# First attention of a two-layer block: both visible triangles of the 128-token window share 128 columns in the softmax

## The reference, cut to what matters

```python
q = jnp.einsum('btd,ndh->btnh', x, q_kernel)          # N = 16 heads of H = 128
kv = jnp.einsum('bsd,ckdh->cbskh', x, kv_kernel)      # K = 8 groups
k, v = (kv[0], kv[1])
q = apply_rope(rms_norm(q, q_norm_scale), positions)
k = apply_rope(rms_norm(k, k_norm_scale), positions)
mask = (j <= i) & (i - j < 128)                       # WINDOW = 128
logits = jnp.einsum('btkgh,bskh->bkgts', qg * ATTN_SCALE, k)
probs = jax.nn.softmax(jnp.where(mask, logits, finfo.min), axis=-1)
enc = jnp.einsum('bkgts,bskh->btkgh', probs, v)
return jnp.einsum('btnh,nhd->btd', enc, out_kernel)
```

## Time and profile before

| | us |
|---|---|
| three runs | 1667.22, 1682.62, 1681.39 |
| median | 1681.39 |
| span of the profiled execution (first to last instruction) | 1677.7 |
| TensorE (PE) busy | 1563.1 (93%) |
| VectorE (DVE) busy | 1115.7 (67%) |
| ScalarE (ACT) busy | 863.7 (51%) |
| GpSimd (POOL) busy | 402.9 (24%) |
| mean granted TensorE clock | 0.945 of full |

### The profile page before, as it was taken

One profiled execution on the slowest core, in us unless ns is written; L12 is line 12 of the kernel. 1 busy time (PEld: TensorE's weight loads), 2 busy tenths in 40 slices (PEclk: granted clock), 3 DMA queues, 4 the chain that ended last, 5 costly groups with the idle time before them and its releaser, 6 DMA issues.

```text
span 1677.7 us, 24009 instructions
## 1 busy us (share of the span) xinstructions
PE 1563.1 (93%) x7538; PEld 1139.9 (68%) x7582; DVE 1115.7 (67%) x2452; ACT 863.7 (51%) x2004; POOL 402.9 (24%) x473
## 2 busy tenths in 40 slices
PE   4999999899999998999999999996999999999898
PEld 3888788778878886677777777774544445444366
DVE  7997798589858983775555555544664756647554
ACT  4777677667766774443323223222443544435466
POOL 4665666466646652000000000000000000000000
PEclk9999999999999998999999999997877989869899
DMA  6000000000000002320000000003000000000001
GB/s 223 2 1 1 1 2 1 3 1 1 1 3 1 2 1 51 96 85 19 1 1 0 0 0 0 0 0 116 1 1 1 1 0 0 0 0 0 0 14 38
DMA packets 15769, 28.04 MB, mean 17 GB/s; under 512 B 2000, under 2 KB 10064, under 8 KB 15152
## 3 DMA queue, kind: packets, MB, share of 16 engines
q1 hardware_dynamic: 15264, 25.98, 4.6%
q0 software_dynamic: 400, 0.78, 0.2%
HBM read 25.44 MB, written 2.10 MB: 16 GB/s over the span
## 4 chain that ended last, share of the span: by engine, by line
PE 74%; DVE 10%; issue 6%; POOL 5%; ACT 4%; DMA 1%; DVEq 0%; ACTq 0%; SPq 0%; POOLq 0%
PE ps L1121 13%; PE ps L1123 13%; PE ps L1122 12%; PE ps L1379 5%; PE ps L1451 4%; PE ps L1174 4%; PE ps L1220 4%; PE ps L1439 4%; PE ps L1426 2%; PE ps L1235 2%; POOL rope L385 2%; PE ps L1512 2%; PE ps L1201 1%; DVE ssum L525 1%; PE ps L1276 1%
## 5 line engine op out<-in xcount | busy, mean ns | idle before, releaser
L1043 ACT ACTIVATE pT<-ps 128x512 f32<-128x512 f32 x256 | 146.1, 597 | 213.9 <-PE ps L1439 212.8
L357 POOL TENSOR_TENSOR ln_rs<-ln_ve,minus_half 128x4 f32<-128x4 f32 x16 | 17.4, 1085 | 978.4 <-DVE ln_ve L421 978.4
L715 DVE TENSOR_REDUCE nm<-ps 128x1 f32<-128x512 f32 x256 | 168.7, 685 | 59.0 <-PE ps L1379 57.5
L1121 PE MATMUL ps<-xnT_lo,w1moe_hi 128*128 128x512 f32 x400 | 178.1, 445 | 2.0 <-DVE w2moe_lo L662 1.8
L974 ACT ACTIVATE moe_act_hi<-sg 128x512 fp32r<-128x512 f32 x100 | 63.3, 633 | 190.5 <-DVE sg L639 190.5
L1122 PE MATMUL ps<-xnT_hi,w1moe_lo 128*128 128x512 f32 x400 | 161.1, 403 | 0.0
L1123 PE MATMUL ps<-xnT_hi,w1moe_hi 128*128 128x512 f32 x400 | 160.0, 400 | 0.0
L385 POOL TENSOR_TENSOR rope<-rope 128x384 f32<-128x384 f32 x128 | 144.3, 1127 | 0.0
L1379 PE MATMUL ps<-kst,qst 64*128 64x512 f32 x256 | 130.1, 526 | 13.3 <-DVE nm L715 7.2
L629 DVE TENSOR_TENSOR sg<-ps,sg 128x512 f32<-128x512 f32 x100 | 69.0, 690 | 97.2 <-ACT sg L994 97.1
L1121 PE MATMUL ps<-wqkv_lo,xnT_hi 128*128 128x512 f32 x256 | 122.1, 477 | 8.6 <-issue 5.6
(11 more groups left out here) (204 smaller groups left out, 3800.1 us busy)
## 6 DMA issues: line engine op xcount, KB each, us to landing
yT<-in_w1moe SPq DMA_DIRECT2D x25, 256.0 KB, 2.6
encT<-in_wqkv SPq DMA_DIRECT2D x8, 512.0 KB, 9.0
w_in<-in_w2moe SPq DMA_DIRECT2D x25, 128.0 KB, 2.7
wo<-in_wo SPq DMA_DIRECT2D x1, 2048.0 KB, 19.5
wm<-in_wm SPq DMA_DIRECT2D x2, 1024.0 KB, 10.8
out_x<-x_res SPq DMA_DIRECT2D x4, 512.0 KB, 2.9
x_res<-in_x SPq DMA_DIRECT2D x1, 1536.0 KB, 15.1
pT<-in_c_pick SPq DMA_DIRECT2D x1, 1024.0 KB, 5.8
```

Source lines behind the costliest of these rows:

```text
L715: V.tensor_reduce(nm1[:, m % 2, t, col:col + 1], ps[:, 2 + i % 2, :], AX.X, ALU.max, negate=True).then_inc(s1_max, 1)
L1043: A(pT1[:, u % 2, 2 * (m % 2) + h, c, :], ps[:, 4 + i % 2, :], ACT.Exp, scale=SCALE1).then_inc(p1_ready, 1)
L1121: MM(out, left[0], right[1], start=first, stop=False)
```

## The change

The two triangles are disjoint, so both fit into 128 columns for the softmax. Scores of a tile with an older triangle: no `window` matmul; the older and the causal products go to two halves of the bank, and VectorE overwrites the causal half where key > query with the older half (`copy_predicated` with the integer mask `older`). Maximum, exponential, normalisation and turning then work on 128 columns a head, always. After turning and copying, GpSimd parts the result again into two zero-filled matrices (`probT_parts`) by two `affine_select` instructions of 128 x 256, and TensorE multiplies each with the values of its tile. A first tile has only the causal triangle, keeps its mask matmul, and needs no parting. VectorE's wait for the scores moves ahead of the reciprocal, and the normalisation becomes one `tensor_tensor`. SP loads one more constant (`older`, 128 KB), and the DMA of `window` becomes that of `causal`.

```diff
@@ gpsimd, attention_step
+                m = n - 7
+                older_too = new and 0 <= m < STEPS and m % TT > 0
+                if older_too:
+                    pool.wait_ge(probT_ready, b * STEPS + m + 1)
+                    if m >= 2:
+                        pool.wait_ge(attended, b * STEPS + m - 1)
                 for h in heads[0:1]:
                     split_weights(h)
+                if older_too and n >= STEPS and not heads:
+                    nc.gpsimd.tensor_tensor(idle[:], minus_half[:, 0:1], minus_half[:, 0:1], ALU.add)
...
                     nc.gpsimd.tensor_tensor(msq[:, s, :], ssum[:, s, :], eps_sum[:], ALU.add).then_inc(meaned, 1)
+                if older_too:
+                    q = m % 2
+                    nc.gpsimd.affine_select(probT_parts[:, q, 0], probT[:, q], [[0, 2], [-1, P]], ALU.is_gt, 0.0,
+                                            base=0, channel_multiplier=1)
+                    nc.gpsimd.affine_select(probT_parts[:, q, 1], probT[:, q], [[0, 2], [1, P]], ALU.is_ge, 0.0,
+                                            base=0, channel_multiplier=-1).then_inc(probT_split, 1)
@@ vector, attention_step
-                    for h in range(2):
-                        ins = V.tensor_scalar(prob[:, m % PROB_RING, h, 0:w], prob[:, m % PROB_RING, h, 0:w], rsums[:, s, h:h + 1],
-                                              None, ALU.mult)
+                    if m % TT:
+                        V.copy_predicated(bank[:, :, 1, :], older[:], bank[:, :, 0, :]).then_inc(merged, 1)
...
+                    V.tensor_tensor(prob[:, m % PROB_RING], prob[:, m % PROB_RING],
+                                    rsums[:, s, :].unsqueeze(2).to_broadcast((P, 2, P)), ALU.mult).then_inc(probn_ready, 1)
...
-                    V.tensor_reduce(nmax[:, s, :], ps[:, 3 + s, :].rearrange("p (h f) -> p h f", h=2)[:, :, 0:w],
-                                    AX.X, ALU.max, negate=True).then_inc(max_ready, 1)
+                    V.tensor_reduce(nmax[:, s, :], bank[:, :, 1, :], AX.X, ALU.max, negate=True).then_inc(max_ready, 1)
@@ scalar, attention_step
-                    kt = slice(1, 4, 2) if m % TT == 0 else slice(0, 4)
-                    A(probT[:, s, kt, :], ps[:, 5, :].rearrange("p (a f) -> p a f", a=4)[:, kt, :], ACT.Copy
+                    A(probT[:, s], ps[:, 5, 0:2 * P].rearrange("p (h f) -> p h f", h=2), ACT.Copy
...
-                        ins = A(prob[:, m % PROB_RING, h, 0:w], ps[:, 3 + s, h * 2 * P:h * 2 * P + w], ACT.Exp,
+                        ins = A(prob[:, m % PROB_RING, h, :], ps[:, 3 + s, (2 * h + 1) * P:(2 * h + 2) * P], ACT.Exp,
@@ tensor, attention_step
-                    pe.wait_ge(probT_ready, k + 1)
+                    if t == 0:
+                        pe.wait_ge(probT_ready, k + 1)
+                    else:
+                        pe.wait_ge(probT_split, b * OLDER_STEPS + with_older(m))
...
-                    else:
-                        MM(ps[:, 3 + s, :], ident_b[:], window[:].rearrange("p h a f -> p (h a f)"),
-                           start=True, stop=False, skip_group_check=True)
...
-                        for part in ((1,) if t == 0 else (0, 1)):
-                            at = 0 if t == 0 else part * P
-                            ins = T(ps[:, 5, (2 * h + part) * P:(2 * h + part + 1) * P],
-                                    prob[:, m % PROB_RING, h, at:at + P], ident[:])
+                        ins = T(ps[:, 5, h * P:(h + 1) * P], prob[:, m % PROB_RING, h, :], ident[:])
```

More of the change, by code:

```diff
@@ L19 @@
 AX = mybir.AxisListType
+I32 = mybir.dt.int32
 P = 128
@@ L97, in build @@
         ident_b = sb("ident_b", [P, P], BF16, part_a)
-        window = sb("window", [P, 2, 2, P], BF16, part_a)
+        idle = sb("idle", [P, 1], where=part_a)
+        causal = sb("causal", [P, 2, P], BF16, part_a)
+        older = sb("older", [P, 2, P], I32, part_a)
         qks = sb("qks", [P, 3, P], where=part_a)
@@ L109, in build @@
         rsums = sb("rsums", [P, 2, 2], where=part_a)
-        prob = sb("prob", [P, PROB_RING, 2, 2 * P], where=part_a)
-        probT = sb("probT", [P, 2, 4, P], where=part_a)
+        prob = sb("prob", [P, PROB_RING, 2, P], where=part_a)
+        probT = sb("probT", [P, 2, 2, P], where=part_a)
+        probT_parts = sb("probT_parts", [P, 2, 2, 2, P], where=part_a)
         encT = sb("encT", [P, HEADS0, SEQ], where=part_a)
@@ L211, in build @@
         wd_loaded = sem("wd_loaded")
-        masks_loaded = sem("masks_loaded")
+        masks_loaded, older_loaded = sem("masks_loaded"), sem("older_loaded")
         out_stored = sem("out_stored")
@@ L280, in heads_next @@
             return (OLD_HEADS_AT.get(n + 1, ()), -1) if old else ((), 0)
+        with_older = lambda m: 3 * (m // TT) + m % TT
+        OLDER_STEPS = GROUPS * (TT - 1)
         weighted_tile = lambda j: -1 if j == 0 else j - 2 if j >= 2 else None
@@ L314, in _ @@
                     sp.dma_start(sin_in, dram["c_sin"]).then_inc(tables_loaded, 16)
+                    sp.dma_start(older[:], dram["c_older"]).then_inc(older_loaded, 16)
             sp.dma_start(x_res[:, TT:NTILES, :], dram["x"][1:BATCHES].rearrange("b (t p) d -> p (b t) d", p=P)
@@ L380, in attention_step @@
                     nc.gpsimd.tensor_tensor(msq[:, s, :], ssum[:, s, :], eps_sum[:], ALU.add).then_inc(meaned, 1)
+                if older_too:
[4 more added lines that the diff above has]
+                                            base=0, channel_multiplier=-1).then_inc(probT_split, 1)
+                if new and n < STEPS:
+                    k, s = b * STEPS + n, n % 2
                     pool.wait_ge(meaned, k + 1)
@@ L918, in attention_step @@
                     m = n - 4
-                    k, s, w = k0 + m, m % 2, (P if m % TT == 0 else 2 * P)
+                    k, s = k0 + m, m % 2
                     act.wait_ge(max_ready, k + 1)
@@ L1173, in attention_step @@
                     for part in parts:
+                        weights = probT[:, s] if t == 0 else probT_parts[:, s, part]
                         ins = MM(ps[:, 6, 0:2 * P], raw[:, (m - 1 + part) % RAW_RING, 3 * P:4 * P],
-                                 probT[:, s, part::2, :], start=part == parts[0], stop=part == 1)
+                                 weights.rearrange("p h f -> p (h f)"), start=part == parts[0], stop=part == 1)
                     ins.then_inc(attended, 1)
@@ L1209, in attention_step @@
                         pe.wait_ge(prob_ready, k - 1)
-                    bank = ps[:, 3 + s, :].rearrange("p (h f) -> p h f", h=2)
+                    bank = ps[:, 3 + s, :].rearrange("p (h a f) -> p h a f", h=2, a=2)
                     if t == 0:
-                        MM(bank[:, :, 0:P], ident_b[:], window[:, :, 1, :], start=True, stop=False,
-                           skip_group_check=True)
-                    else:
-                        MM(ps[:, 3 + s, :], ident_b[:], window[:].rearrange("p h a f -> p (h a f)"),
-                           start=True, stop=False, skip_group_check=True)
+                        MM(bank[:, :, 1, :], ident_b[:], causal[:], start=True, stop=False, skip_group_check=True)
                     for h in range(2):
                         for part in ((1,) if t == 0 else (0, 1)):
-                            at = 0 if t == 0 else part * P
-                            ins = MM(bank[:, h, at:at + P], qkT[:, m % QK_RING, h, :],
-                                     qkT[:, (m - 1 + part) % QK_RING, 2, :], start=False,
+                            ins = MM(bank[:, h, part, :], qkT[:, m % QK_RING, h, :],
+                                     qkT[:, (m - 1 + part) % QK_RING, 2, :], start=t > 0 and h == 0 and part == 0,
                                      stop=h == 1 and part == 1, skip_group_check=True)
@@ L1619 @@
     qi, kj = np.arange(P)[:, None], np.arange(P)[None, :]
-    masks = np.where(np.stack([kj > qi, kj <= qi], 1), np.float32(0), np.float32(-1e30))
-    arrays["c_window"] = np.ascontiguousarray(np.broadcast_to(masks[:, None], (P, 2, 2, P)))
+    masks = np.where(kj <= qi, np.float32(0), np.float32(-1e30))
+    arrays["c_causal"] = np.ascontiguousarray(np.broadcast_to(masks[:, None], (P, 2, P)))
+    arrays["c_older"] = np.ascontiguousarray(np.broadcast_to((kj > qi).astype(np.int32)[:, None], (P, 2, P)))
     feat = np.arange(FT * P)
```

30 lines of the change are left out of this document (21 added, 9 removed).

## The result

The changed kernel takes 1849.54 us (median of 4 runs, 1841.18 to 1860.08) against 1677.43 (1667.22 to 1682.62) for the kernel before, by runs of both on the same chip: ratio 1.1044, 95% interval 1.0973 to 1.1115. The forecast was 1933 in a range of 1835 to 2035. The profiled execution took 1852.63 us with a span of 1850.9, which is 173.2 above the span of before.

What follows compares the result with a forecast made beforehand. TensorE was taken to bound the first attention, until selections close a longer loop through four engines. 1681.4 + 215 for the loop - 10 outside its stretches + 47 for the clock = 1933 us, range 1835 to 2035.

Steps and rivals of the forecast that it cites:

- the loop: First attention: projection, copy, square, sum, msq, two selections, product, next projection; 4.91 + 2S us an interval against today's 4.13.
- the stretches: First attention, steps 8 to 31 of each batch: groups of four tiles take 24.27 instead of 15.31 us, +215 us.
- rival 1: First attention: selections cheap and clock holds; 1833 us with S = 0.57, 1855 with S = 0.725; chance 0.22.
- the clock: TensorE's granted clock falls after pauses in half of the 72 long intervals: +47 us, bounds nothing to +150.
- S: Time of one GpSimd selection, two per tile with an older triangle: taken as 0.94 us.
- the short interval: Fourth interval of a group, with a first tile's product and no selections to wait for: 3.9 us.
- Outside the stretches: Steps 0 to 7 and 32 to 39: 24 tiles save 0.43 us each, -10 us; +10 if cover is gone.
- What the change removes: TensorE, 96 tiles with an older triangle: mask and two turns, 0.43 us a tile, 41 us if TensorE stayed the bound.
- VectorE at nothing: VectorE's edits, with copy_predicated taken as 0.42 us, sum to -0.2 us, at worst +0.2; costed at nothing.
- faster: First attention: selections are hidden and TensorE keeps its pace less 0.43 us a tile, 1640 us; chance 0.02.
- the clock falling in nearly every interval: First attention: clock falls almost always, 2036 us, or selections take 1.3 us or more, about 1985; chance 0.20.
- rival 4: First attention: VectorE and GpSimd's loop alone, lengthened by selections to 5.7 us, binds; 1805 us; chance 0.05.

Runs made afterwards that it cites:

- the kernel with both loops cut: Changed kernel with selections made a step earlier, between rms and rotation, and VectorE's qkn of the previous tile behind ssum: 1649.66 us, ratio to before 0.9823.
- the second experiment: Changed kernel with the two selections behind the rotation instead of between msq and rms, in steps with a projection: 2102.52 us (one run).

## Why the prediction was right, and where its sizes were off

- **The mechanism was right.** "The loop is longer than TensorE's work before a selection has cost anything": three other places of the selections and their near-removal all move the time the way the loop says, though the sizes missed in two of them. Its length without selections was put at 4.91 and is 4.8 (5.34 - 0.57 measured, and 5.77 - 0.96). The product waits for the second selection 72 times in the stretches, as forecast, mostly by 1.82 us instead of 2 to 3.
- **The number was less right than the range suggests.** 1850 is 83 us below the forecast, outside the inner range of 1880 to 1985 that got half of the chances, and 15 us inside the edge of the outer one. It lies between the prices of rival 1, 1833 and 1855, and that rival is half right too: selections were even cheaper than it said, but the clock didn't hold. Two other errors cancel in the sum: the clock was put 21 us too high and the steps outside the stretches 22 too low. What is left is the stretches, 80 too high, and 4 in the time before.
- **The term that was mis-sized is S.** It was taken as 0.94 from L367, bounded below by the 0.57 of `msq`. Measured:

```profile
L399 POOL TENSOR_SCALAR_AFFINE_SELECT probT_parts<-probT x96: 398/522/761, 54.0 to 813.6; 128x256 f32<-128x256 f32 x96
L401 POOL TENSOR_SCALAR_AFFINE_SELECT probT_parts<-probT x96: 397/517/523, 54.5 to 813.9; 128x256 f32<-128x256 f32 x96
```

  0.52, and 0.48 from start to start. By the prediction's other links that makes the loop 5.87 (5.77 measured). A group at VectorE's sum is 3 x 5.77 + 3.62 = 20.93 instead of 3 x 6.79 + 3.9 = 24.27. Of the 3.34 us between them, 2.76 are the six selections at 0.46 less each, 0.3 the other links and 0.28 the short interval; times 24 that is 66, 7 and 7 us of the 80 by which the 215 was too high. The estimate of 0.4 that the prediction made by the rule of the GPSIMD Engine Reference of the Trainium skill (Engine selection), that one-input operations run roughly at line rate, was the better price: 0.397 is the least measured.
- **The lower bound was no bound.** `msq` isn't 0.57 by itself. Right behind `ssum` it runs beside VectorE's L569, which has two SBUF inputs and lasts 0.56. In the kernel with both loops cut, the same VectorE instruction (L572 there) is nearly over when `msq` starts, and `msq` takes 0.19 (0.198 in the median of all 128, against 0.567 before):

```profile
385.39 0.55 DVE L572 TENSOR_TENSOR rope<-raw,cos 128x384 f32<-128x384 f32 x1
...
385.84 0.19 POOL L389 TENSOR_TENSOR msq<-ssum,eps_sum 128x3 f32<-128x3 f32 x1
```

  So the row from which I took the bound most likely held a wait that the trace counts as duration. That the wait is for a port shared with VectorE is argued from such pairs, not shown by an experiment of its own.
- **The clock** was put at 47 us, half of the intervals; it is 26. Most pauses were 1.82 us and not 3.1. The bound "all of them" at 2.1 each was approached only with the pauses of 3.5 us in the second experiment.
- **Outside the stretches** I expected -10, or +10 "if the cover is gone". It is about +12: the cover was too thin. 20 of the 92 waits, some 20 us, lie outside, against the 10 saved. In the steps after the last projection:

```profile
385.14 1.13 PE L1217 MATMUL ps<-probT_parts,raw 128*128 128x256 f32 x4 [1.58 <-POOL probT_parts L401]
...
388.01 1.13 PE L1217 MATMUL ps<-probT_parts,raw 128*128 128x256 f32 x4 [0.30 <-POOL probT_parts L401]
...
394.18 1.13 PE L1217 MATMUL ps<-probT_parts,raw 128*128 128x256 f32 x4 [1.14 <-POOL probT_parts L401]
```

- **What the change removes** held: 0.43 us a tile was forecast, and TensorE's step in the kernel with both loops cut is 3.68 instead of 4.13. **VectorE at nothing** held too. `copy_predicated` takes 0.403, near the 0.42 taken, and VectorE waits for others in the loop. **The rivals**: faster and no difference fell, and so did the clock falling in nearly every interval; rival 4, the loop of VectorE and GpSimd, wasn't the bound but appeared when the selections were made a step earlier. The sum with the measured sizes, 1677.7 + 135 + 26 + 12, gives the span of 1851.

## What to carry to other kernels

Ask of an added instruction first where it stands in its engine's queue and what the instruction ahead of it waits for; a wait inherited from a neighbour closed a loop of 4.8 us here that the 0.96 us of work would not have. Two instructions moved past one gave back 146 of 172 us, and with the selections a step earlier and a second loop cut the same change became 1.8% faster than the kernel before. An engine at 24% of the page can be at 69% in the stretch that matters, and the next bound after a cut is the loop that was just shorter. A short instruction's row is no lower bound of its cost when a neighbour runs beside it.

## What the runs showed of the hardware that I had not expected

- The same `affine_select` of 128 x 256 floats on GpSimd took 0.40 us alone, 0.52 beside VectorE's L572 and L573, and 0.76 when it started 0.06 us after VectorE's `qkn` (all of them two-input instructions from SBUF). VectorE pays as well: L573 lasts 0.56 beside a selection; the same instruction takes 0.35 in the mean in the kernel before (L533).

```profile
465.48 0.35 DVE L572 TENSOR_TENSOR rope<-raw,sin 128x192 f32<-128x192 f32 x1
...
465.75 0.56 DVE L573 TENSOR_TENSOR rope<-raw,sin 128x192 f32<-128x192 f32 x1
```

  This agrees with the rule of the Trainium skill's SBUF — State Buffer (Who interferes with whom) that a GpSimd instruction reading SBUF and such a VectorE one keep each other out.
- An `affine_select` of 128 x 2 took 0.18 us at least, against 0.40 for 128 x 256, so nearly half of the 0.40 doesn't depend on the columns. Beside VectorE's L572 and L573 it took 0.30.
- A pause of 1.82 us was followed by a fall of TensorE's clock in some intervals and not in others; seven useless matmuls in the pause gave 25 us back.
